# Attention steps with four 64x64 score tiles at a step's end, value products one step later, and the attention division between the two row maxima

## What is computed

```
h = layernorm(x)
qh, kh, vh = split_heads(h @ Wq.T), split_heads(ctx @ Wk.T), split_heads(ctx @ Wv.T)
scores = einsum("bhqd,bhkd->bhqk", qh, kh) * sqrt(8)
attn = softmax(where(mask, -1e9, scores))
x = x + merge_heads(attn @ vh) @ Wo.T
x = x + moe(layernorm(x))      # 16 experts, top 2 of a router, and one shared expert
```

## Time and profile before

| what | value |
|---|---|
| median of 3 runs | 190.49 us (189.46 to 192.41) |
| the profiled execution's own time | 190.56 us |
| span from its first to its last instruction | 188.7 us |
| mean granted TensorE clock | 0.985 |
| PE, DVE, ACT, POOL busy, share of the span | 92%, 85%, 69%, 47% |

### The profile page before, as it was taken

How to read it: one execution, slowest core, us unless ns; L and a number is a source line. 1 busy time by engine, 2 the same in 40 slices (tenths; PEclk the granted TensorE clock), 3 DMA queues, 4 the chain that set the end, 5 groups by cost and what they waited for, 6 DMA issues and landing times.

```text
span 188.7 us, 4275 instructions
## 1 busy us (share of the span) xinstructions
PE 173.1 (92%) x1305; PEld 124.9 (66%) x1305; DVE 161.4 (85%) x501; ACT 130.2 (69%) x292; POOL 89.2 (47%) x146
## 2 busy tenths in 40 slices
PE   7887889787999999999999799999999999999963
PEld 7763455455666666666677476788878877788741
DVE  5569999997999999999984899988988899889961
ACT  3195797776899999999889566565556555665631
POOL 7049997369888888888698850400000000000000
PEclk9999999999999999999999999999999999999985
DMA  5999200000000000000003423432534153315201
GB/s 105 288 332 386 96 2 2 3 0 2 3 0 5 0 0 0 0 0 5 0 1 94 147 106 109 118 115 92 152 118 154 70 158 136 130 63 161 62 2 56
DMA packets 12128, 15.43 MB, mean 82 GB/s; under 512 B 1744, under 2 KB 6608, under 8 KB 11984
## 3 DMA queue, kind: packets, MB, share of 16 engines
q1 hardware_dynamic: 10800, 13.79, 22.8%
q10 hardware_dynamic: 1312, 1.46, 2.8%
HBM read 14.06 MB, written 1.18 MB: 81 GB/s over the span
## 4 chain that ended last, share of the span: by engine, by line
PE 55%; DVE 23%; issue 7%; ACT 4%; DMA 4%; POOL 3%; ACTq 1%; DVEq 0%; POOLq 0%
PE bank L1092 31%; PE bank L1039 8%; PE bank L1021 4%; DMA mhalf<-mask_half 4%; PE bank L1030 4%; DVE hid L904 4%; DVE smax L827 4%; DVE prob L848 3%; ACT hid_hi L667 2%; DVE k_all L769 2%; PE bank L1010 2%; PE bank L1000 2%; DVE stats L701 1%; POOL k_blk L455 1%; PE bank L990 1%
## 5 line engine op out<-in xcount | busy, mean ns | idle before, releaser
L1039 PE MATMUL bank<-k_blk,q_blk 128*128 128x512 f32 x64 | 33.9, 614 | 1.3 <-POOL k_blk L455 1.1
L658 ACT ACTIVATE sig<-bank 128x512 f32<-128x512 f32 x36 | 21.5, 599 | 19.1 <-PE bank L1092 18.7
L455 POOL TENSOR_TENSOR k_blk<-k_all,consts_sb 128x512 f32<-128x512 f32 x32 | 33.2, 1058 | 0.0
L667 ACT CAST hid_hi<-hid 128x512 fp32r<-128x512 f32 (+1 forms) x37 | 22.4, 609 | 12.0 <-DVE hid L904 11.9
L1092 PE MATMUL bank<-xt_hi,w_hi 128*128 (+1 forms) x72 | 29.3, 407 | 0.2 <-ACT sig L658 0.2
L896 DVE TENSOR_TENSOR hid_lo<-hid,hid_hi 128x512 fp32r<-128x512 f32 (+1 forms) x37 | 25.1, 680 | 4.3 <-ACT hid_hi L667 4.1
L1092 PE MATMUL bank<-xt_hi,w_lo 128*128 (+1 forms) x72 | 28.2, 392 | 0.0
L1092 PE MATMUL bank<-xt_lo,w_hi 128*128 (+1 forms) x72 | 28.2, 392 | 0.0
L602 ACT ACTIVATE prob<-prob,exp_scale 128x512 f32<-128x512 f32 x32 | 23.8, 744 | 2.9 <-DVE prob L848 2.9
L887 DVE TENSOR_TENSOR hid_u<-sig,bank 128x512 f32<-128x512 f32 x32 | 21.8, 682 | 3.9 <-PE bank L1092 2.5
L904 DVE TENSOR_TENSOR hid<-hid_u,cb 128x512 f32<-128x512 f32 x32 | 23.0, 718 | 0.0
(11 more groups left out here) (117 smaller groups left out, 333.2 us busy)
## 6 DMA issues: line engine op xcount, KB each, us to landing
cb<-comb_rows SPq DMA_DIRECT2D x64, 128.0 KB, 2.9
w_moe_sb<-w_moe SPq DMA_DIRECT2D x1, 1296.0 KB, 10.3
ctxt_sb<-ctx_t SPq DMA_DIRECT2D x4, 256.0 KB, 8.7
xt_sb<-x_t ACTq DMA_DIRECT2D x4, 256.0 KB, 8.4
x_sb<-x SPq DMA_DIRECT2D x4, 256.0 KB, 11.0
out<-x_sb SPq DMA_DIRECT2D x3, 256.0 KB, 3.1
w_moe_sb<-w_moe SPq DMA_DIRECT2D x1, 432.0 KB, 7.9
w_att_sb<-w_att SPq DMA_DIRECT2D x1, 264.0 KB, 3.9
```

Source lines behind the costliest of these rows:

```text
L455: last = nc.gpsimd.tensor_tensor(k_blk[p][:, g, :, :], k_all[:, bass.ds(t, 1), g, :].broadcast_to([P, HG, S]), hmask_sb.rearrange("p (h o) ...
L658: nc.scalar.activation(sig[r][:, :], gate_ps[r][:, :], ACT.Silu).then_inc(s_sig, 1)
L667: nc.scalar.copy(hid_hi[k][:, cols], hid[k][:, cols]).then_inc(s_hid_hi, 1)
L1039: nc.tensor.matmul(score_ps[g][:, :], q_blk[q][:, g, :, :].rearrange("p b s -> p (b s)"), k_blk[q][:, g, :, :].rearrange("p h s -> p (h s) ...
```

## The change

Scores: instead of two products over 128 rows with half of the query block zeroed, a step issues four products of 64 rows by 64 columns, each with 512 moving columns, one for each pair of batch and head group, placed on the four quarters of the array (`tile_position=(b * S, hg * S)`). Bank b now holds batch b, with the head group in the partition half. `q_blk` has half the elements (a copy of the queries by a multiplication with ones; the half mask goes), and `exp_scale` becomes one tile per bank, written by four small instructions instead of one. The scores are those of tile t+2 instead of t+1, and stand at the end of the step, behind the router; they wait for both subtractions, and the step waits for `k_blk` of the same step (`s_blk`) ahead of the router. The value products of tile t-1 stand at the start of step t (16 products as before, in another order of columns). On ACT `pvt_sb` moves ahead of `prob_t`, the second `prob_t` ahead of `att_t`, and the two exponentials stand side by side (they remain two instructions). On DVE the division stands between the first subtraction and the second row maximum. After the last step the value products of tile 15 are issued ahead of `gate(0, 1)`, and their copy on ACT ahead of the first `silu`.

```
@@ q_block, k_blocks and exp_scale on POOL
-                nc.gpsimd.tensor_tensor(exp_scale[:, tiles], rstd1[p][:, :], any_scale[:, tiles],
-                                        ALU.mult).then_inc(s_escale, 1)
+                for turned in range(2):
+                    for b in range(BPT):
+                        src = slice(b * S, (b + 1) * S)
+                        hg = 1 - b if turned else b
+                        last = nc.gpsimd.tensor_tensor(exp_scale[b][hg * S:(hg + 1) * S, tiles], rstd1[p][src, :],
+                                                       any_scale[src, tiles], ALU.mult)
+                    last.then_inc(s_escale, 1)
+                    pool.wait_ge(s_escale, 2 * g + turned + 1)
...
-                    q_blk[p][:, :, :, :],
-                    q_all[:, bass.ds(t, 1), :, :].rearrange("p o g (c s) -> p (o g) c s", c=1).broadcast_to([P, 2, BPT, S]),
-                    half_mask_sb.rearrange("p (o b e) -> p o b e", o=1, e=1).broadcast_to([P, 2, BPT, S]), ALU.mult)
+                nc.gpsimd.tensor_tensor(q_blk[p][:, :, :], q,
+                                        ones_sb[:, :].rearrange("p (o s) -> p o s", o=1).broadcast_to([P, 2, S]),
+                                        ALU.mult)
@@ ACT step
+                if on(1) and not (isinstance(t, int) and t == TILES):
+                    values_to_sbuf(t - 1)
                 if on(0):
                     transposed(0)
...
+                if on(0):
+                    transposed(1)
                 if on(1):
                     act.wait_ge(s_at, t)
                     nc.scalar.copy(att_t[q][:, :], at_ps[:, 0:P]).then_inc(s_at_sb, 1)
-                if on(0):
-                    transposed(1)
@@ PE step
+                def scores(n, r):
...
+                    for b in range(BPT):
+                        rows = slice(b * S, (b + 1) * S)
+                        for hg in range(2):
+                            last = nc.tensor.matmul(score_ps[b][hg * S:(hg + 1) * S, :], q_blk[r][rows, hg, :],
+                                                    k_blk[r][rows, hg, :, :].rearrange("p h s -> p (h s)"), start=True,
+                                                    stop=True, tile_position=(b * S, hg * S))
+                        last.then_inc(s_score[b], 1)
...
+                    values(t - 1, q)
...
-                    values_as_rows(t - 1)
                 if on(0):
                     transposes(0)
-                if on(-1):
-                    scores(1)
-                else:
+                if not on(-1):
                     pe.wait_ge(s_sub[1], TILES)
                     up(0, 0)
                 if on(1):
-                    if once and t == TILES - 1:
-                        pe.wait_ge(s_ct_sb, 1)
-                    attention_transposed(t - 1, q)
+                    values_as_rows(t - 1)
                 if on(0):
                     transposes(1)
                 if on(2):
                     norm_transposed(t - 2, p)
                 if on(1):
+                    if once and t == TILES - 1:
+                        pe.wait_ge(s_ct_sb, 1)
+                    attention_transposed(t - 1, q)
                     output_projection(t - 1, q)
...
+                if on(-2) and not (once and t < 0):
+                    pe.wait_ge(s_blk, t + 2)
                 if on(2):
                     router(t - 2, p)
+                if on(-2) and not (once and t < 0):
+                    scores(t + 2, p)
```

More of the change, by code:

```diff
@@ L116, in build_program @@
         veps1 = [sb(f"veps1_{p}", [P, GT]) for p in range(2)]
-        exp_scale = sb("exp_scale", [P, TILES])
+        exp_scale = [sb(f"exp_scale{b}", [P, TILES]) for b in range(BPT)]
         neg_half = sb("neg_half", [P, GT])
         eps_sb = sb("eps_sb", [P, GT])
+        ones_sb = sb("ones_sb", [P, S])
         pause = sb("pause", [P, 8])
-        q_blk = [sb(f"q_blk{p}", [P, 2, BPT, S]) for p in range(2)]
+        q_blk = [sb(f"q_blk{p}", [P, 2, S]) for p in range(2)]
         k_blk = [sb(f"k_blk{p}", [P, 2, HG, S]) for p in range(2)]
@@ L458, in k_blocks @@
                         hmask_sb.rearrange("p (h o) -> p h o", o=1).broadcast_to([P, HG, S]), ALU.mult)
-                last.then_inc(s_blk, 1)
+                last.then_inc(written, 1)
             mask_ctx(1)
@@ L841, in step @@
                         ALU.mult).then_inc(s_att, 1)
+                if on(1) and not on(-1):
+                    attention()
                 if on(-1):
@@ L844, in step @@
                         if g == 1:
+                            if on(1):
+                                attention()
                             row_max(1)
@@ L984, in keys_values, with values @@
                 last.then_inc(s_v, 1)
+            def values(t, p):
+                pe.wait_ge(s_vblk, t + 1)
+                for h in range(2):
+                    pe.wait_ge(s_pt_sb[h], t + 1)
+                    for hg in range(2):
+                        for c in range(GT):
+                            last = nc.tensor.matmul(
+                                pvt_ps[c * PW:(c + 1) * PW, hg * P + h * S:hg * P + (h + 1) * S],
+                                v_blk[p][:, h, hg * GT + c, :], prob_t[p][:, h * GT + c, hg * S:(hg + 1) * S],
+                                start=True, stop=True, tile_position=(0, c * PW))
+                last.then_inc(s_pvt, 1)
             def values_as_rows(t):
@@ L1022, in transposes @@
                     last.then_inc(s_pt[h], 1)
[L1024 to L1046 removed]
+                def scores(n, r):
+                    if once and n == 0:
+                        pe.wait_ge(s_blk_first, 1)
+                    else:
+                        pe.wait_ge(s_const, 16)
+                        for b in range(BPT):
+                            pe.wait_ge(s_sub[b], n)
+                    for b in range(BPT):
+                        rows = slice(b * S, (b + 1) * S)
+                        for hg in range(2):
+                            last = nc.tensor.matmul(score_ps[b][hg * S:(hg + 1) * S, :], q_blk[r][rows, hg, :],
+                                                    k_blk[r][rows, hg, :, :].rearrange("p h s -> p (h s)"), start=True,
+                                                    stop=True, tile_position=(b * S, hg * S))
+                        last.then_inc(s_score[b], 1)
+                if once and t < 1:
+                    if t == 0:
+                        pe.wait_ge(s_blk, 1)
+                    scores(t + 1, q)
+                elif not on(-1):
                     pe.wait_ge(s_sub[0], TILES)
@@ L1049, in step @@
                     weights_as_rows(0)
+                if once and t == 0:
+                    pe.wait_ge(s_k_raw, GROUPS - 1)
                 if on(1):
@@ L1152, in _ @@
             pipeline(pe, step)
+            values(TILES - 1, 1)
             gate(0, 1)
```

70 lines of the change are left out of this document (22 added, 48 removed).

## The result

| | before | after |
|---|---|---|
| median of 4 runs, us | 190.50 (189.46 to 192.41) | 197.91 (197.17 to 198.68) |
| ratio, with its 95% interval | | 1.041 (1.034 to 1.048) |
| profiled execution, us (its span) | 190.56 (188.7) | 197.47 (195.6) |

What follows compares the result with a forecast made beforehand. PE, full at 4.52 us a step, was taken as the bound. Start +0.8, loop +2.6 and end +1.6 on 190.56 gave 195.6, stated against the median as 195.5 us, 2.6% slower; range 191.3 to 201.0.

Steps and rivals of the forecast that it cites:

- PE's own work: Score products in each step: four quarters run together in 0.94 us, so PE's work falls by 0.94 to about 3.6.
- pairs in turn: Rival on the score products: quarters overlap only partly, set costs 1.88 us, total 206; chance 0.11 including all four singly.
- The new loop through PE and ACT: In each step, two round trips from PE to ACT in a row: 4.78 us instead of 4.52, +2.6 over ten periods.
- What DVE could do at best: DVE's own period in the loop: 4.52 - 0.20 + 0.11 = 4.43 us, no bound under 4.78.
- Before the loop: Start: four scale operations instead of one (+0.71), smaller q_blk, later scores; +0.8 us taken, ends 0.2 and 1.2.
- Behind the loop: Step 15 up to gate(0, 1): trailing values of tile 14 and bare waits; +1.6 us, ends 0.8 and 2.2.
- The change doesn't do all it says: Rival on ACT: the two exponentials remain two instructions and save nothing by being neighbours; already in the forecast, no separate chance.
- The rule against the change: Tiling mode switches on PE drain it, 0.11 us each, three a step instead of two: step 4.89, total 196.6.
- The sum: Whole kernel: 190.56 + 0.8 + 2.6 + 1.6 = 195.6, forecast 195.5 us, 2.6% slower.
- What would show it: Signs in the profile: PE below 85% busy in the loop, two idle places, period 4.7 to 4.9, table load near 106.
- Rivals: Alternatives to the forecast: score quarters overlapping poorly (0.11), a shorter loop bound by DVE (0.16), exponentials saving nothing (in forecast).
- DVE's floor: Rival in the loop: values 0.43 and scores 0.86 make it 4.40, DVE's 4.43 rules, total 191.4; chance 0.16.

Runs made afterwards that it cites:

- the first two runs: The changed kernel with the order of before (old_order, 191.9 us), and with two whole-array score products (full_scores, 206.23 us).
- old_late_tr1: The old_late kernel with PE's second transposes moved ahead of the transpose of the attention; 190.31 us, ratio 0.999.
- filler: The changed kernel with ten unused products on PE, once, in the long wait ahead of norm_transposed near 45 us; 196.34 us, ratio 1.031.
- old_order: The changed kernel's four 64x64 score products and scale operations, with the order of before on PE, ACT and DVE; 191.9 us, ratio 1.011.
- best: The old_late_tr1 kernel with the negated mean moved from DVE to POOL and xn2 ahead of the first turned weights on ACT; 190.41 us, ratio 0.999.
- late_scale: The changed kernel with the last group's four scale operations moved on POOL to behind the key blocks of step 3; 195.18 us, ratio 1.022.
- old_late: The old_order kernel with the last group's scale operations moved later on POOL, as in late_scale; 190.43 us, ratio 1.003.
- filler2: The changed kernel with more unused products than filler, also in the smaller PE waits of steps 2 and 3; 196.39 us, ratio 1.031.
- full_scores: The changed kernel's order, with the scores again as two whole-array products of a masked query block; 206.23 us, ratio 1.083.

## Why the prediction was right, point by point

- **PE's own work.** The four score products as one set was right: 1.02 us to the next instruction against the 0.94 taken, and nowhere near the 1.88 of pairs in turn. Against the forecast loop that is +0.08.
- **The new loop through PE and ACT.** Right in kind: the chain has the links that were named, in their order, and the first two runs show that the order makes it. The sum was 4.78; the step between 68.32 and 73.24 took 4.92, most others 4.84 to 4.85. Link by link: values 0.59 instead of 0.73, the transposes' end 0.66 instead of 0.60, `xn2` to PE 0.12 instead of 0.06, `norm_transposed` to the next 0.17 instead of 0.11, `output_projection` 0.43 instead of 0.39, router 0.30 instead of 0.24. The durations were read in rows in which PE was never idle; the products that start on a waiting PE, `norm_transposed` and `output_projection`, cost 0.06 and 0.04 more than there. Ten periods cost 3.1 instead of 2.6: the new step is 4.88 on average instead of 4.78, which is 1.0 more, and the old one 4.57 instead of 4.52, which takes 0.5 back.
- **What DVE could do at best.** Not tested, and read 0.1 too long. The term had no part in the sum, since DVE is no bound at 4.78. The earlier trace rows show 0.20 of idle time ahead of the logits, but the start-to-start distance there (73.14 to 73.62) is 0.48, and it is 0.20 where the logits don't wait (`old_late_tr1`), so DVE gives away 0.28 a step: an estimate from these rows is 4.52 - 0.28 = 4.24 for DVE's order of before, and 4.35 for the changed one with its 0.11. The 4.44 of `old_late_tr1` lies near the forecast 4.43 by chance: its DVE has the order of before and still waits. So that "whatever PE saves, DVE gives back all but a fraction" is not shown, and it is not why the tiles gain nothing. In the order of before PE waits for the division on DVE, which stands behind the first maximum, and DVE for PE's router; with that wait filled, PE waits for ACT.
- **Before the loop.** The start came 1.0 later, 0.8 was taken; the four scale operations take 42.52 - 41.46 = 1.06 where one took 0.15, so +0.9 instead of +0.71: each pair was mis-sized by 0.1. That 1.0 lies so near 0.8 is partly luck: counted from the first score product it is 1.5, of which about 0.2 is the fall of the clock, already under way at 45.1 (in `filler`, at full clock up to there, it is 30.59 us instead of 30.80). What the step missed altogether is the fall of the granted clock behind the longer wait, 1.9 us. It was named among what would show the forecast wrong, but for the loop, where PE idles 13% in short pieces and the clock stayed at 1.00; it fell ahead of it, where PE stands still for longer.
- **Behind the loop.** 1.5 measured, 1.6 taken. Nothing takes the delay up, as forecast; that it shrinks to 6.9 us at the very end is the fall of the clock in the profiled execution of before.
- **The change doesn't do all it says.** As forecast: two exponentials in a row are 1.35 us of ACT, as two instructions.
- **The rule against the change.** The Trainium skill (TensorEngine Tiling (Array Packing), Tiling Modes) has a drain at a switch of mode, which the earlier trace rows put at 0.11: the link scores to values is 1.02 instead of 0.94, and 1.02 again in `old_order`, where full-array products follow. That is 0.08, near the 0.11 of the earlier trace rows, but no run separates the drain from an overlap short of four. The Trainium skill's 3.07 for four row tiles (TensorE: Matmul & The Clock Gate, Measured speedup vs the span model) would have made the link an estimated 1.22; the trace gives 4 x 0.94 / 1.02 = 3.7.
- **The sum.** 195.5 against 197.9. The terms were off by +0.2 (start), +1.9 (clock), +0.5 (loop), -0.1 (last scores to the gate), -0.1 (behind) and -0.5 (the end, where the clock of before fell): +1.9 against the profiled execution, which lies 0.4 below the median. The clock after is the largest term of the miss, but by one execution of each kernel.
- **What would show it.** Right: the two idle times and their releasers, DVE's wait for the residual, the span of the scores (1.09). Slightly off: PE at 87% in the loop, not under 85%, and the table load at 109.06, not near 106, by the clock and the loop.
- **Rivals.** Pairs in turn did not happen. The changed order never came near DVE's floor; the values' 0.43 and the scores' 0.86 on which that case stood were 0.59 and 1.02.

## What to carry to other kernels

When an engine is full, freeing it is worth only what the loops between the engines leave. Here four orders of the same work with PE at 87 to 92% (after, `old_order`, `old_late_tr1`, `best`) took 4.44 to 4.9 us a step, though by the estimate above DVE, the next fullest engine, could do 4.24 to 4.35; what held them was each time a chain that goes from PE to another engine and back. So read the chain, and not only the busy shares, and see whether the new order leaves every wait something to stand behind. Two round trips in a row to the same other engine, with everything later behind them, are a loop whose length is the sum of its links, and it can be added up from the rows of the old trace to within 3%. Small operations that a start must pass cost their own length there (1.07 us in `late_scale`), and may cost a fall of the clock besides. A waits view leaves out the short waits: compare start-to-start distances before saying that an engine has none. And where the clock can fall, compare the granted clock of both executions over their whole length before a difference of one or two microseconds is given to a cause.

## What the hardware showed that was not expected

The granted clock can fall to the 1.2 GHz level in the middle of a kernel, and the length of the wait ahead of it does not settle whether it does. In one profiled execution each, it fell behind 2.87 us without work after, behind 1.82 in `late_scale`, and behind 0.97 and 1.09 us in `old_late_tr1`; it did not fall behind 1.57 and 1.42 in `old_late`, behind 0.81 and 0.98 before, or behind 1.97 us near 28 us after, where it did fall in `filler2`. In `filler` it fell 3 us after the long wait had been filled, behind three short ones (0.64, 0.35, 0.18). Of the thirteen profiled executions only those of before and `old_late` show no fall between 24 and 55 us, and before has one at its end. It stayed low for 3.4 us in `filler` and 6.8 us after. It cost between 0.9 us (this step in `old_order` and, without a fall, in `old_late`: 5.97 and 5.06) and 2.4 us (`full_scores`), since the work under it is what the next step waits for. It is in the scatter of the kernel before as well: of its 49 executions beside the experiments, those with a mean granted clock of 0.998 or more took 188.8 to 190.0 us, those with 0.979 or less 190.9 to 191.5. What besides idle time decides it stays open.

Four 64x64 float32 products of 512 columns on the four quarters of the array ran as one set: eight passes in 1.02 us, where one whole-array product, two passes, takes 0.94.
